# Sending row maxima in halves of eight tiles, and following the strips by 12 steps instead of 20

## The reference, cut to what matters

```python
x: (4, 2048, 256) float32, 16 heads of 16, WINDOW = 128, N_GLOBAL = 1
q, k, v = x @ Wq.T, x @ Wk.T, x @ Wv.T                 # per head
attend = (|i - j| <= 128) | (i < 1) | (j < 1)           # band, first row, first column
logits = where(attend, q @ k.T * 0.25, -inf)
out = softmax(logits) @ v @ Wo.T
x = x + out                                             # between the two mixture steps
```

## Time and profile before

| | us |
|---|---|
| median of the three timed runs | 1012.6 |
| lowest and highest | 1011.14 and 1017.5 |
| the profiled execution, its own time | 1013.68 |
| its span, first to last instruction | 1012.1 |
| A alone (20 steps) | 46.5 to about 93 |
| A and B together (236 steps) | about 93 to 895 |
| B alone (20 steps) and the last projections | 895 to about 972 |
| second routing, to the end | 972 to 1012.1 |

### The profile page before, as it was taken

One profiled execution on the slowest core, in us unless ns is written; L12 is line 12 of the kernel. 1 busy time (PEld: TensorE's weight loads), 2 busy tenths in 40 slices (PEclk: granted clock), 3 DMA queues, 4 the chain that ended last, 5 costly groups with the idle time before them and its releaser, 6 DMA issues. The chain is left out here.

```text
span 1012.1 us, 50930 instructions
## 1 busy us (share of the span) xinstructions
PE 873.1 (86%) x21696; PEld 617.4 (61%) x21697; DVE 798.3 (79%) x2873; ACT 680.0 (67%) x1500; POOL 471.1 (47%) x748
## 2 busy tenths in 40 slices
PE   2789988999899999998999999989999998889910
PEld 1445655666677676666677676666686676655610
DVE  6399888988887889989777889988787888842456
ACT  2414767886676678886766678876676777778610
POOL 5211546654444446555444546654544545555400
PEclk9799999999999999999999999999999999999955
DMA  5222223422123243422123343412123231110200
GB/s 174 76 95 70 76 70 106 128 69 68 58 67 104 94 138 108 110 67 68 60 70 99 93 138 103 117 59 68 65 78 97 93 121 57 58 46 23 87 22 4
DMA packets 92523, 83.55 MB, mean 83 GB/s; under 512 B 17280, under 2 KB 91264, under 8 KB 92288
## 3 DMA queue, kind: packets, MB, share of 16 engines
q1 hardware_dynamic: 92288, 80.21, 25.0%
HBM read 20.65 MB, written 8.39 MB: 29 GB/s over the span
## 5 line engine op out<-in xcount | busy, mean ns | idle before, releaser
L939 ACT ACTIVATE probs<-bank 128x384 f32<-128x384 f32 (+1 forms) x1024 | 466.8, 481 | 182.0 <-PE bank L834 175.8
L1129 DVE CUSTOM_DVE_ANT_0 bank<-bank,con 128x288 f32<-128x288 f32 x1024 | 497.8, 520 | 101.7 <-PE bank L811 93.0
L811 PE MATMUL bank<-k_stack,q_stack 96*32 96x288 bf16 x4096 | 322.5, 293 | 27.1 <-DVE row_max L1129 23.8
L834 PE MATMUL bank<-q_stack,k_stack 99*32 99x288 bf16 (+2 forms) x4096 | 316.9, 288 | 12.3 <-ACT probs L939 9.8
L852 PE MATMUL bank<-probs,v_sb 128*32 128x128 f32 x5888 | 304.6, 277 | 2.6 <-ACT o_raw L946 1.3
L988 POOL TENSOR_SCALAR_AFFINE_SELECT probs<-probs 128x512 f32<-128x512 f32 x240 | 154.5, 644 | 230.8 <-ACT probs L939 229.2
L852 PEld LDWEIGHTS bank<-probs,v_sb 128*32 128x32 f32 x5888 | 186.9, 112 | 43.3 <-issue 11.0
L811 PEld LDWEIGHTS bank<-k_stack,q_stack 96*32 96x32 bf16 x4096 | 121.0, 96 | 113.5 <-DVE row_max L1129 63.7
L993 POOL TENSOR_SCALAR_AFFINE_SELECT probs<-probs 128x512 f32<-128x512 f32 x240 | 152.2, 634 | 32.8 <-ACT probs L939 32.8
L707 PE MATMUL bank<-xnT,wqk_sb 128*32 128x256 f32 x2048 | 166.1, 398 | 0.0
L834 PEld LDWEIGHTS bank<-q_stack,k_stack 99*32 99x32 bf16 x4096 | 119.0, 96 | 71.8 <-ACT probs L939 48.9
(11 more groups left out here) (114 smaller groups left out, 803.1 us busy)
## 6 DMA issues: line engine op xcount, KB each, us to landing
q_stack<-pieces SPq DMA_DIRECT2D x384, 64.0 KB, 2.6
k_stack<-pieces SPq DMA_DIRECT2D x384, 64.0 KB, 2.6
x_ring<-in_x SPq DMA_DIRECT2D x28, 512.0 KB, 4.6
out_x<-x_ring SPq DMA_DIRECT2D x16, 512.0 KB, 3.8
attn<-in_x SPq DMA_DIRECT2D x4, 512.0 KB, 6.7
wback_sb<-in_wback SPq DMA_DIRECT2D x8, 256.0 KB, 5.7
q_stack<-neg_max SPq DMA_DIRECT2D x48, 16.0 KB, 2.3
probs<-in_wqk SPq DMA_DIRECT2D x1, 512.0 KB, 5.5
```

The lines of the kernel that those rows point to most:

```text
L811: last = pe.matmul(a_ring[i % len(a_ring)][SP * s:SP * (s + 1), 0:WIN], q_stack[g % 2][0:KROWS, h, q:q + SP], k_stack[g % 2][0:KROWS, h, q ...
L834: last = pe.matmul(b_ring[i % len(b_ring)][SP * s:SP * (s + 1), start:final], k_stack[g % 2][0:SROWS, h, WINDOW + P * j + SP * s:WINDOW + ...
L939: act.activation(probs[:, j % 4, h, c0:c1], b_ring[i % len(b_ring)][:, c0:c1], ACT.Exp, scale=LOGIT_SCALE).then_inc(S["exp_ready"], 1)
L1129: dve.tensor_tensor_reduce(out=a_ring[i % len(a_ring)][:, 0:WIN], in0=a_ring[i % len(a_ring)][:, 0:WIN], in1=mask, scale=1.0, scalar=con[: ...
```

## The change

The row maxima of a group are handled in two halves of eight tiles. KEY0, TURN_MAX, MAX and EXP0 come twice for a group, at steps 16g + 8 and 16g + 16. Each works on 32 columns of `row_max` or 32 partitions of `neg_max` instead of 64. The three pieces lie in one array `neg_max` [32, 3, 128]; one DMA from SP writes it to a small DRAM array `max_rows` (event MAX), and a second one (MAX_IN, three quarters later), behind a wait for the first, reads it back into the half rows of `q_stack`. TensorE waits for the first half ahead of B of a group's tile 0 and for the second ahead of tile 7.

`LAG_B` becomes 12, `LAG_PV` 15 and `LAG_TURN` 19. The output, VALUES and late FIRST events move eight steps ahead with them, the early FIRST events four, WBACK six. STACK moves from step t + 5 (fourth quarter) to t + 4 (second quarter), or t + 3 (fourth quarter) for the second chunk. The stretch in which the four parts of QK lie in neighbouring quarters (`apart`) moves by eight steps as well.

```diff
-        LAG_B, LAG_PV = NT + 4, NT + 7
+        LAG_B, LAG_PV = NT // 2 + 4, NT // 2 + 7
-        MAX_STACKED = 16 * 3
+        MAX_STACKED = 16
+        HALF = NT // 2
-                    late = NT * NG * (b + 1) + (24 if b < nb - 1 else LAG_TURN - 15) + 4 * c
+                    late = NT * NG * (b + 1) + (16 if b < nb - 1 else LAG_TURN - 15) + 4 * c
-                    apart = 1 if 10 <= t % (NT * NG) < 44 else 2
+                    apart = 1 if 2 <= t % (NT * NG) < 36 else 2
-                    end(t + 5, 3, "STACK", n, c)
-                end(NT * n + NT - 1, 3, "KEY0", n)
-                begin(NT * n + NT, 0, "TURN_MAX", n)
-                opening(NT * n + NT, 1, "MAX", n)
-                opening(NT * n + NT + 1, 0, "EXP0", n)
+                    end(t + (3 if c == 1 else 4), 3 if c == 1 else 1, "STACK", n, c)
+                for half in range(2):
+                    t = NT * n + HALF * (half + 1)
+                    end(t - 1, 3, "KEY0", n, half)
+                    begin(t, 0, "TURN_MAX", n, half)
+                    opening(t, 1, "MAX", n, half)
+                    end(t + 1, 0, "MAX_IN", n, half)
+                    opening(t + 1, 0, "EXP0", n, half)
-                            begin(r + 10 + 2 * u, part, "VALUES", b, u, part)
+                            begin(r + 2 + 2 * u, part, "VALUES", b, u, part)
-                end(r - 10 if b else -24, 0, "WBACK", b)
-                for stage, t in enumerate((-5, -1, 3, 7, 11, 15, 23, 27, 31)):
+                end(r - 16 if b else -24, 0, "WBACK", b)
+                for stage, t in enumerate((-9, -5, -1, 3, 7, 11, 15, 19, 23)):
...
                         elif kind == "MAX":
-                            g, = n
-                            sp.wait_ge(S["max_piece"], 3 * g + 3)
-                            for i in range(3):
-                                sp.dma_start(q_stack[g % 2][KROWS + i:KROWS + i + 1, :, :], neg_max[i][:, :])\
-                                  .then_inc(S["max_stacked"], 16)
+                            g, half = n
+                            sp.wait_ge(S["max_piece"], 3 * (2 * g + half) + 3)
+                            sp.dma_start(max_rows.rearrange("i (r p) -> r i p", p=P), neg_max[:, :, :])\
+                              .then_inc(S["max_out"], 16)
+                        elif kind == "MAX_IN":
+                            g, half = n
+                            sp.wait_ge(S["max_out"], 16 * (2 * g + half + 1))
+                            sp.dma_start(q_stack[g % 2][KROWS:SROWS, :, P * HALF * half:P * HALF * (half + 1)],
+                                         max_rows.rearrange("i (h n) -> i h n", h=HG)).then_inc(S["max_stacked"], 16)
...
-                            if j == 0 and h == 0:
-                                pe.wait_ge(S["max_stacked"], MAX_STACKED * (g + 1))
+                            if j in (0, HALF - 1) and h == 0:
+                                pe.wait_ge(S["max_stacked"], MAX_STACKED * (2 * g + (1 if j == 0 else 2)))
```

More of the change, by code:

```diff
@@ L81, in build @@
         s0T = sb("s0T", [P, NT, H])
-        row_max = sb("row_max", [P, 2, HG, NT])
+        row_max = sb("row_max", [P, 2, 2, HG, NT // 2])
+        max_rows = nc.dram_tensor("max_rows", (3, NT // 2 * HG * P), BF16, kind="Internal").ap()
         p0_arg = sb("p0_arg", [P, NT, HG])
         p0 = sb("p0", [P, 2, NT, HG])
-        neg_max = [sb(f"neg_max{i}", [NT * HG, P], BF16) for i in range(3)]
-        neg_rest = sb("neg_rest", [NT * HG, P])
+        neg_max = sb("neg_max", [NT // 2 * HG, 3, P], BF16)
+        neg_rest = sb("neg_rest", [NT // 2 * HG, P])
         logits = [sb(f"logits{i}", [P, B * NT, E]) for i in range(2)]
@@ L1114, in _ @@
                         elif kind == "KEY0":
-                            g, = n
-                            dve.wait_ge(S["a_free"], NT * HG * (g + 1))
+                            g, half = n
+                            dve.wait_ge(S["a_free"], HG * (NT * g + HALF * (half + 1)))
                             dve.wait_ge(S["s0_ready"], g // NG + 1)
                             head = HG * (g % NG)
-                            maxima = row_max[:, g % 2, :, :].rearrange("p h t -> p t h")
-                            dve.tensor_tensor(maxima, maxima, s0T[:, :, head:head + HG], ALU.max)\
+                            maxima = row_max[:, g % 2, half, :, :].rearrange("p h t -> p t h")
+                            dve.tensor_tensor(maxima, maxima, s0T[:, HALF * half:HALF * (half + 1), head:head + HG],
+                                              ALU.max)\
                                .then_inc(S["key0_ready"], 1)
@@ L1135, in _ @@
                             head = HG * (g % NG)
-                            if g:
-                                dve.wait_ge(S["max_stacked"], MAX_STACKED * g)
-                                dve.wait_ge(S["p0_ready"], g)
-                            dve.wait_ge(*filled("TURN_MAX", g))
-                            top = bank_of("TURN_MAX", g)[0:NT * HG, 0:P]
-                            dve.tensor_scalar(neg_max[0][:, :], top, -1.0, None, ALU.mult)\
+                            if m:
+                                dve.wait_ge(S["max_stacked"], MAX_STACKED * m)
@@ L1142, in _ @@
+                            dve.wait_ge(*filled("TURN_MAX", g, half))
+                            top = bank_of("TURN_MAX", g, half)[0:HALF * HG, 0:P]
+                            dve.tensor_scalar(neg_max[:, 0, :], top, -1.0, None, ALU.mult)\
                                .then_inc(S["max_piece"], 1)
-                            dve.wait_ge(S["max_piece"], 3 * g + 1)
+                            dve.wait_ge(S["max_piece"], 3 * m + 1)
                             dve.scalar_tensor_tensor(out=neg_rest[:, :], in0=top, scalar=-1.0,
-                                                     in1=neg_max[0][:, :], op0=ALU.mult, op1=ALU.subtract)\
-                               .then_inc(free_sem("TURN_MAX", g), 1)
@@ L1158, in _ @@
-                            dve.memset(p0_arg[:, 0, :], MASKED)
-                            dve.wait_ge(S["p0_diff"], g + 1)
-                            dve.memset(p0_arg[0:1, 1, :], MASKED).then_inc(S["p0_arg_ready"], 1)
+                                                     in1=neg_max[:, 0, :], op0=ALU.mult, op1=ALU.subtract)\
+                               .then_inc(free_sem("TURN_MAX", g, half), 1)
+                            dve.wait_ge(*emptied("TURN_MAX", g, half))
+                            dve.tensor_copy(neg_max[:, 1, :], neg_rest[:, :]).then_inc(S["max_piece"], 1)
@@ new lines, in _ @@
+                            dve.wait_ge(S["max_piece"], 3 * m + 2)
+                            dve.tensor_tensor(neg_max[:, 2, :], neg_rest[:, :], neg_max[:, 1, :],
+                                              ALU.subtract).then_inc(S["max_piece"], 1)
+                            dve.wait_ge(S["key0_ready"], m + 1)
+                            if m >= 2:
+                                dve.wait_ge(S["p0_ready"], m - 1)
+                            at = slice(HALF * half, HALF * (half + 1))
@@ new lines, in _ @@
+                            last = dve.tensor_tensor(
+                                p0_arg[:, at, :], s0T[:, at, head:head + HG],
+                                row_max[:, g % 2, half, :, :].rearrange("p h t -> p t h"), ALU.subtract)
+                            if half == 0:
+                                last.then_inc(S["p0_diff"], 1)
+                                dve.wait_ge(S["p0_diff"], g + 1)
+                                dve.memset(p0_arg[:, 0, :], MASKED)
+                                last = dve.memset(p0_arg[0:1, 1, :], MASKED)
@@ L1161, in _ @@
+                            last.then_inc(S["p0_arg_ready"], 1)
                         elif kind == "OUT":
```

43 lines of the change are left out of this document (18 added, 25 removed).

## The result

The changed kernel takes 1026.15 us (median of 4 runs, 1025.94 to 1029.61), the one before 1012.22 beside it (1011.14 to 1017.5): a ratio of 1.0135, with a 95% interval of 1.0094 to 1.0177. Timed a second time, on another chip, it took 1029.21 against 1010.07, a ratio of 1.0187 (1.0147 to 1.0228). So it is slower by 14 to 19 us, where 10.7 were forecast. The profiled execution took 1026.0 us, its span is 1024.3.

The account below looks back on a forecast made before the run. No engine was taken as full: short work handed through small rings binds the middle, so added VectorE time soon reaches the others. -11.3 + 21 + 1 = +10.7 us gave a forecast of 1023 us, range 1005 to 1039.

Parts of the forecast that it names:

- The steps of B alone: Near the end of the run, eight steps with B alone and no projection beside them vanish: -16.3 us.
- Steps 12 to 20: In the head, these steps of A get B and PV beside them, 2.94 us each instead of 2.31: +5.0 us.
- VALUES under A alone: In the head, VALUES moves eight steps earlier into steps 2 to 12, costed at nothing; at worst 5.0 us more.
- Part 1: Eight steps less over the whole run, B 12 steps behind A instead of 20: -11.3 us, bounds -16.3 and -6.
- rival 3: Faster: heavy fill work behind B moves away from A's norms, shortening the fullest steps; 1002 us, chance 0.13.
- Part 2: Sixteen added rounds of maxima cost VectorE 1.3 us per group, fully paid: +21 us, bounds 10 and 35.
- TensorE stands at its turns, ScalarE runs dry behind it: At TURN_MAX, TensorE waits 1.3 us for KEY0 with matmuls queued behind; about 40 us over 32 turns.
- Part 3: Two serial DMAs through DRAM, 2.3 to 2.6 us each, covered before B of tiles 0 and 7, barely: +1 us.
- Part 4: SP's queue: STACK's twelve issues wait behind the new stand of some 3 us, covered: cost and gain nothing.
- the half-hidden rounds: Rival: in the middle, idle VectorE time hides half the added rounds, costing 10 us; no change, 1012 us, chance 0.25.
- Two hops hold B up: Rival: at 4 us per DMA, tile 7 stands at TensorE's queue in most groups; 1039 us, chance 0.15.
- The busiest steps get shorter: Mechanism of rival 3: projections, VALUES and FIRST leave the steps with A's norms, returning 10 us; chance 0.13.

Follow-up runs that it names:

- one_round: Changed kernel with only the first half's round of maxima per group, second eight tiles' maxima left out: 1008.28 us, ratio 0.997 to the kernel before.
- one_round_later: Changed kernel with only the first half's round per group, at step 16g + 9, and the first chunk's STACK one step later: 990.88 us, ratio 0.9766.
- pad_dve: Changed kernel with four additions of 128 x 160 on VectorE, four steps behind each of the 32 rounds: 1057.69 us, ratio 1.0453.
- pool_pieces: Changed kernel with second and third piece, key-0 difference and its memsets on GpSimd instead of VectorE: 1016.47 us, ratio 1.0077.
- turn_later: Changed kernel with TURN_MAX and MAX one quarter later in 24 places of 32: 1027.87 us, ratio 1.0194.
- third_hop: Changed kernel with one more serial 24 KB DMA, DRAM to DRAM, between write and read of the maxima: 1045.4 us, ratio 1.0343.
- half0_later: Changed kernel with the first half's round one step later, at 16g + 9, STACK kept in place: 1080.48 us, ratio 1.0692.
- later_stack_pool: Changed kernel with first half's round and first chunk's STACK one step later, second and third piece and key-0 difference on GpSimd: 1012.84 us, ratio 0.9996.
- after_again: The changed kernel unaltered, timed again on another chip as the measure for other runs there: 1029.21 us, ratio 1.0187.

## Why the prediction came out as it did

The forecast of 1023 us is 3 us below the 1026.15 measured, and the sign is the one given as likeliest. By the second timing, +19 against +10.7, it is 8 us short. Step by step:

- **The steps of B alone, -16.3.** Right: the end is 16.2 us shorter, and 18.7 in one_round.
- **Steps 12 to 20, +5.0.** Right: +6.1, and +5.1 in one_round. 24.52 us are 3.1 a step, "near 2.9".
- **VALUES under A alone, nothing.** Wrong by a little: steps 0 to 12 are 1.2 us longer, 2.5 in one_round. The bound was 5.
- **Part 1 in sum, -11.3.** This is the weakest step. one_round measures -3.0 by the ratio, -7.5 by the spans of the two profiles. The end came out 2.4 us better than priced, steps 0 to 12 took 2.5 and the middle 4.3, both put at nothing. Why the middle takes 4.3 is not shown: it is what is left of larger changes of both signs, because the fill work moved by eight steps (rival 3, below). What the sum has no term for at all is the place of the round: one step later is worth 20 us over sixteen rounds (one_round_later), more than the whole of part 1.
- **Part 2, +21, "VectorE's ledger, fully paid".** The ledger is right (20.9 us), and the sum is near (16.7 to 22), but the reason isn't the one given. Added VectorE time is paid at two thirds (28.5 of 42 in pad_dve) and given back at a third to six tenths (6 to 11 of 18 in pool_pieces), and by place from nothing to double. The second half's rounds at steps 192, 208, 224 and 240, from four steps around each in the changed kernel and in one_round, follow. Columns as in the earlier trace rows; the changed kernel first, then one_round.

```profile
700.04:715.28 15.24, 14.02 (x391) 9.96 (x393) 12.82 (x46) 9.92 (x23) 7.23 (x12) 1.00 0.15 47
757.58:773.36 15.78, 15.78 (x354) 10.74 (x351) 12.33 (x43) 10.96 (x25) 6.64 (x10) 1.00 0.23 69
823.27:836.82 13.55, 12.78 (x353) 9.16 (x349) 12.82 (x55) 11.08 (x26) 7.52 (x14) 1.00 0.16 51
874.27:889.96 15.69, 12.92 (x261) 8.40 (x261) 12.35 (x44) 8.72 (x21) 6.81 (x10) 0.78 0.15 47
```

```profile
688.49:702.18 13.69, 13.61 (x390) 10.25 (x392) 11.41 (x41) 9.90 (x22) 7.24 (x12) 1.00 0.25 80
744.48:759.93 15.45, 15.45 (x353) 10.77 (x350) 11.02 (x37) 10.78 (x24) 6.64 (x10) 1.00 0.44 124
809.54:822.08 12.54, 12.29 (x352) 9.28 (x348) 11.76 (x49) 10.91 (x25) 8.02 (x14) 1.00 0.28 94
860.85:872.15 11.30, 9.72 (x260) 6.91 (x260) 10.44 (x38) 8.36 (x20) 6.81 (x10) 1.00 0.27 87
```

  That is 1.55, 0.33, 1.01 and 4.39 us for one round. The cheap one stands where one_round leaves VectorE the most room (busy 11.02 of 15.45 us) and TensorE none, ahead and behind: there the step is as long as TensorE's work, and the round vanishes beside it. Elsewhere TensorE has 0.8 to 2.8 us of idle time in the changed kernel, where one_round has 0.1, 0.3 and, in the last row, 1.6. The last row has the granted clock at 0.78 of full speed in its stretch, where one_round has 1.00, so not all of it is the round's own.
- **"TensorE stands at its turns, ScalarE runs dry behind it".** Seen (35.9 us in 27 turns; "about 40" in 32 were forecast), but as the cause it falls: turn_later took 22.8 us of the stand away and the time stayed.
- **Part 3, two hops, +1.** Right within what can be told: no gap ahead of B of tile 0 or 7 over 0.4 us, and third_hop shows cover for less than one hop more. The hop of 24 KB into DRAM lands in 2.2 us; 2.3 to 2.6 were taken. The profile has no landing for the read. The Trainium skill gives its fixed cost of about 2.0 us ("DMA: Bandwidth & Descriptors", the anatomy of one DMA) for DMAs issued from GpSimd, and these are issued from SP; the estimate of 2.1 that was made from it lies near the row all the same.
- **Part 4, SP, nothing.** Right for the change as it is: the wait for `b_full` fell from 121.4 to 14.0 and nobody gained. The warning that belongs to it was too weak, though: half0_later shows that one step of a round's place puts twelve issues between write and read and costs 51 us.

Of the rivals, the half-hidden rounds have the right mechanism in some places (0.33 us at step 208) and the wrong sum. "Two hops hold B up" doesn't happen in the changed kernel. "The busiest steps get shorter" has its sign in the trace and not its gain: the busiest steps moved. In the second to fourth entry the fullest four steps were those around step 32; now they are those around step 24, eight steps earlier, as long as before and with the same 351 matmul instructions. The kernel before around step 96 (step 32 of the second entry), then the changed kernel around steps 88 and 96:

```profile
338.84:356.79 17.95, 16.03 (x351) 11.09 (x343) 15.24 (x58) 12.78 (x29) 8.29 (x14) 1.00 0.32 100
```

```profile
328.02:345.89 17.87, 16.02 (x351) 11.07 (x343) 15.21 (x58) 12.80 (x29) 8.31 (x14) 1.00 0.29 97
362.22:375.76 13.54, 12.78 (x353) 9.20 (x349) 12.81 (x53) 11.07 (x26) 7.51 (x14) 1.00 0.19 61
```

So the objection in the prediction, that the fill work only changes places, holds. That the forecast came as near as 3 us is partly luck: part 1 came out 8 us worse than priced by the ratios, part 2 between 4 us better and 1 worse, and against +10.7 stand 14 to 19 us measured, by which of the two timings one takes.

What stays open: where the missing 4 to 8 us of part 1 lie, why the added round at step 56 costs 3.2 us and more with B 20 steps behind (the norms are beside it, but no run separates them from it), and the gain that later_stack_pool didn't bring. A single DMA from the pieces to the stack, without DRAM, and B 16 steps behind weren't tried.

## What to carry to other kernels

A small serial step (VectorE, TensorE's turn, VectorE, DMA, B) is priced by where it stands, not by its instructions: see what is queued directly ahead of it on the engine it starts on, and try it one step later before its work is cut down; here that was worth about 1 us a round (14 to 19 us over sixteen), as much as an added round costs. When an event is moved by one step, go through every queue it is on: SP's order decided between 1012 and 1080 us. And when a sum of stages agrees with a trace, run one part alone before believing it: the largest stage of this one agreed, and added VectorE time was not paid in full as the sum had it.

## What the runs showed of the hardware

A write of 24 KB from 32 partitions into DRAM was no dearer than a move of 16 KB inside SBUF: 1.4/2.2/3.8 us from issue to landing (min/median/max) against 2.1/2.3/3.9; 24 KB from DRAM to DRAM (third_hop) took 1.9/2.0/3.7. The issue of the write takes 0.33 us, while that of the read with its three rows takes 0.75 (ns min/median/max):

```profile
L633 SPq DMA_DIRECT2D max_rows<-neg_max x32: 308/327/343, 66.6 to 925.7; - x32
L638 SPq DMA_DIRECT2D q_stack<-max_rows x32: 729/746/851, 68.5 to 927.1; - x32
```

TensorE's clock is granted at half (1.2 of 2.4 GHz) in short stretches ahead of the last 50 us in every kernel here: 37.5 us in sum in the profiled execution of the changed kernel, 47.8 in that of after_again, the same program, whose span is 3.4 us longer. Whether the one comes from the other isn't shown; two traces of one kernel differ by that much, and I trust a difference between single places of two kernels only where both rows show the clock at 1.00.
